# Expert steps of 256 rows instead of 128, with the first layer's weights stationary and split a step ahead, and the last norm's sums on GpSimd

## The chip, the core and the metric

The kernel runs on one core of a Trainium2 chip. Its engines run their own queues in order and meet at semaphores: TensorE (PE; PEld is its weight load), VectorE (DVE), ScalarE (ACT), GpSimd (POOL), and SyncE (SP), which mostly issues DMA. The metric is the device time of one execution in microseconds.

## What is computed

A transformer block after the norm-last scheme: attention with linear cost, layer norm, a mixture of experts (8 experts, each token goes to its best two), layer norm. 4 x 2,048 tokens of width 256, all in float32.

```python
q = relu(x @ Wq.T + bq); k = relu(x @ Wk.T + bk); v = x @ Wv.T + bv      # 16 heads of 16
q_ = concat(q * sin, q * cos); k_ = concat(k * sin, k * cos)
kv = einsum('nld,nlm->ndm', k_, v)
z = 1.0 / maximum(einsum('nld,nd->nl', q_, k_.sum(axis=1)), EPS)
x = layernorm(x + (einsum('nld,ndm->nlm', q_, kv) * z) @ Wo.T + bo)
topv, topi = top_k(x @ router_w.T, 2); w = softmax(topv)
for e in range(8):                                                       # w1: 512 x 256, w2: 256 x 512
    out += gate[:, e:e + 1] * (gelu(x @ w1[e].T) @ w2[e].T)
x = layernorm(x + out)
```

## The kernel before, in words

**Precision.** Every float32 product runs as three products of rounded numbers: each operand is split into a high part (a copy by ScalarE or GpSimd into the type fp32r) and a low part (the original less the high part, by VectorE or GpSimd); `PASSES` names high x high, high x low, low x high. So each split of an operand is two instructions, on two engines, ahead of the product.

**First half.** Tokens go through in 32 pairs of 128. TensorE makes keys, values and queries; the state of a batch is complete after its 8 pairs, so that the attention of a pair follows 9 pairs behind. Each pair then has a chain: attention product for each of its two tiles (`attend`), combination of the sine and cosine parts and division (`add_sin_part`, `normalise_attention`), transposes (`attention_transposed`), output projection (`project_out`), residual and norm, routing (`choose`, `gates`), places of rows in the experts' lists (`rank`, `positions`). GpSimd scatters each token's row twice into `expert_rows` in HBM, one region for each expert. Beside this GpSimd splits the experts' weights half by half from a raw buffer `wraw`; the last expert's are split at the change to the second half.

**Second half.** The experts work in 135 steps of 128 rows. A table made from the counts gives each step its expert and its place; a first table is made after 20 pairs, a second one when all are counted, and steps from `FULL_STEPS` on use it. SyncE gathers a step's rows from `expert_rows` into one of `NXG` = 8 buffers `xg` as soon as `freed` says that the results that lay in it have been sent. TensorE turns the rows (`rows_transposed`, a step ahead), multiplies them with the first layer (`hidden`: the rows stand still, the weights move past as 512 columns), turns the hidden rows (`hidden_transposed`) and multiplies with the second layer (`outputs`, of the step before). ScalarE copies the rows' high part, applies GELU and copies the hidden rows' high part; VectorE makes the low parts and adds the gated outputs to the rows (`gated`). GpSimd sends them to `token_rows` in HBM (`send`).

**Hooks.** The last eight pairs, and what is left of the 24th, are worked on between the expert steps: `hook(s)` gives for each step the pair and which of its six stages stands behind this step, in the code of every engine alike. The order of each queue is thus written by hand.

**Last norm.** From step 92 on, `ticks(s)` spread the second norm over the steps, four tiles of 128 tokens in three steps: SyncE loads a chunk (4 tiles, 1 MB) of `token_rows` into `z2`, VectorE adds the two rows of each token (`tile_sum`) and takes statistics, GpSimd computes the deviation's power (`deviation`), ScalarE scales and stores.

## Time and profile before

| | |
|---|---|
| median of three runs | 849.87 us (847.88 to 852.35) |
| profiled execution, span of its instructions | 841.6 us; its own total is not listed, the runs' median lies 8.3 above the span |
| TensorE busy | 793.9 us, 94% |
| VectorE, ScalarE, GpSimd busy | 566.7, 461.0, 434.3 us |
| mean granted TensorE clock | 0.984 of full |
| chain that ended last | TensorE 61% of the span, of it second layer 23%, first layer 22%, hidden transposes 7%, row transposes 4% |

A busy share is a mean over both halves. The chain is followed back from the last instruction: what stands in it sets the time where it stands.

### The profile page before, as it was taken

The page shows a single profiled execution, that of the slowest core. Times are in us where ns is not written, and L with a number is a line of the kernel's source. Part 1 is how long each engine was busy: PE and PEld are TensorE (multiplying, and loading weights), DVE is VectorE, ACT ScalarE, POOL GpSimd, SP SyncE. Part 2 cuts the span into 40 slices and gives each one's busy share as a digit, 9 for nine tenths or more (in the row PEclk, how much of TensorE's full clock was granted, in tenths as well). Part 3 has the DMA queues.
Part 4 walks back from the last instruction along what each step waited for, and adds up shares of the span by engine and source line. Part 5 has one row for each costly group of instructions (what it writes and reads, how often), then busy time and mean ns, then how long its engine had stood idle before and what let it go on. Part 6 is the DMA issues. An engine that isn't in the chain of part 4 may idle for free.

```text
span 841.6 us, 22076 instructions
## 1 busy us (share of the span) xinstructions
PE 793.9 (94%) x6684; PEld 732.7 (87%) x6684; DVE 566.7 (67%) x1816; ACT 461.0 (55%) x1044; POOL 434.3 (52%) x545
## 2 busy tenths in 40 slices
PE   4999999999999979999999999999999999999990
PEld 4887899899899969999999999989999999999980
DVE  3435788888888857766676666664444477777773
ACT  4656677667777644454444445434444446556663
POOL 3985477677677755544444454542222234444442
PEclk9999999999999989999999999999999999999995
DMA  6444033333333333323323323233322545666644
GB/s 205 160 150 127 26 102 122 113 110 108 108 103 102 98 131 117 119 90 96 99 93 96 108 88 105 87 100 107 99 78 74 179 133 193 228 226 223 220 175 173
DMA packets 56468, 106.64 MB, mean 127 GB/s; under 512 B 9261, under 2 KB 37551, under 8 KB 54448
## 3 DMA queue, kind: packets, MB, share of 16 engines
q1 hardware_dynamic: 41296, 63.25, 24.5%
q0 software_dynamic: 12624, 33.84, 11.0%
q10 hardware_dynamic: 2448, 8.26, 2.7%
q8 instruction: 58, 0.95, 0.5%
q14 instruction: 42, 0.34, 0.1%
HBM read 61.91 MB, written 44.32 MB: 126 GB/s over the span
## 4 chain that ended last, share of the span: by engine, by line
PE 61%; DMA 1%; DVE 1%; ACT 1%; issue 1%; SPq 0%; POOLq 0%; POOL 0%; ACTq 0%
PE PS L737 23%; PE PS L725 22%; PE PS L755 7%; PE PS L714 4%; PE PS L578 2%; PE PS L630 2%; DMA z<-token_rows 1%; PE PS L601 0%; PE PS L541 0%; DMA token_rows<-xg 0%; DMA expert_rows<-rows,idx 0%; PE PS L632 0%; DMA xg<-expert_rows 0%; ACT rows L862 0%; PE PS L614 0%
## 5 line engine op out<-in xcount | busy, mean ns | idle before, releaser
L1683 POOL DMA_INDIRECT token_rows<-xg x135 | 135.1, 1000 | 271.6 <-DVE xg L1407 251.1
L737 PEld LDWEIGHTS PS<-w,hT 128*128 128x128 f32 x1620 | 211.5, 190 | 12.0 <-issue 1.9
L725 PE MATMUL PS<-w,xgT 128*128 x810 | 222.0, 409 | 0.0
L737 PE MATMUL PS<-w,hT 128*128 x1620 | 217.2, 284 | 0.8 <-ACT hT L993 0.8
L725 PEld LDWEIGHTS PS<-w,xgT 128*128 128x128 f32 x810 | 143.2, 189 | 24.6
L1602 POOL DMA_INDIRECT expert_rows<-rows,idx x128 | 133.9, 1046 | 56.1 <-issue 27.8
L993 ACT ACTIVATE hT<-PS 128x512 fp32r<-128x512 f32 x135 | 80.8, 598 | 135.6 <-PE PS L755 135.6
L989 ACT ACTIVATE hg<-PS 128x512 f32<-128x512 f32 x135 | 80.7, 598 | 120.6 <-PE PS L725 120.3
L1471 DVE TENSOR_TENSOR hT<-PS,hT 128x512 fp32r<-128x512 f32 x135 | 93.4, 692 | 75.9 <-ACT hT L993 75.9
L1399 DVE TENSOR_TENSOR xgT<-PS,xgT 128x256 fp32r<-128x256 f32 x135 | 56.9, 422 | 77.8 <-ACT xgT L961 76.3
L755 PE MATMUL PS<-cst,hg 128*128 128x128 f32 x540 | 81.1, 273 | 0.0
L541 PE MATMUL PS<-wk,xs 128*128 128x264 f32 x384 | 64.3, 304 | 14.5 <-DVE wv L1340 8.4
L1407 DVE SCALAR_TENSOR_TENSOR xg<-PS,xg 128x256 f32<-128x256 f32 x135 | 65.0, 482 | 14.0 <-PE PS L737 4.9
L541 PEld LDWEIGHTS PS<-wk,xs 128*128 128x128 f32 x384 | 51.2, 192 | 21.2 <-ACT vs L853 11.8
L578 PE MATMUL PS<-sts,qs 128*128 128x272 f32 x384 | 60.7, 294 | 2.7 <-DVE sts L1091 2.4
L755 PEld LDWEIGHTS PS<-cst,hg 128*128 128x128 f32 x540 | 62.7, 141 | 0.1
L714 PE MATMUL PS<-cst,xg 128*128 128x128 f32 x270 | 52.3, 276 | 5.0 <-DMA xg<-expert_rows 4.0
L541 PE MATMUL PS<-wv,xs 128*128 128x256 f32 x384 | 56.9, 285 | 0.0
L614 PE MATMUL PS<-xs,wq 128*128 128x256 f32 x384 | 56.8, 294 | 0.0
L630 PE MATMUL PS<-wo,aT 128*128 128x264 f32 x384 | 56.5, 286 | 0.0
L578 PEld LDWEIGHTS PS<-sts,qs 128*128 128x128 f32 x384 | 52.0, 191 | 4.0 <-issue 3.0
L961 ACT ACTIVATE xgT<-PS 128x256 fp32r<-128x256 f32 x135 | 51.2, 379 | 3.4 <-PE PS L714 3.4
(179 smaller groups left out, 1272.8 us busy)
## 6 DMA issues: line engine op xcount, KB each, us to landing
xg<-expert_rows SPq DMA_DIRECT2D x135, 130.0 KB, 2.1
z<-token_rows SPq DMA_DIRECT2D x15, 1024.0 KB, 7.8
xraw<-in_xT SPq DMA_DIRECT2D x32, 256.0 KB
xtok<-in_x SPq DMA_DIRECT2D x32, 256.0 KB, 2.8
out_y<-z ACTq DMA_DIRECT2D x15, 512.0 KB, 3.4
wraw<-in_w1T SPq DMA_DIRECT2D x7, 512.0 KB, 3.9
wraw<-in_w2T SPq DMA_DIRECT2D x7, 512.0 KB, 4.0
token_rows<-xg POOLq DMA_INDIRECT x135, 2.6
```

The source lines that it names most:

```text
L541: return nc.tensor.matmul(PS[:, bank, 0:columns], xs[:, rep % 2, a, k, h * P:(h + 1) * P], weights[:, b, k, :], start=(n == 0), stop=(n == ...
L578: mm = nc.tensor.matmul(PS[:, bN + half, 0:2 * NW], qs[:, a, half, h * P:(h + 1) * P], sts[:, b, half].rearrange("p a b -> p (a b)"), star ...
L630: nc.tensor.matmul(PS[:, bank, 0:KE], aT[:, a, k, h * P:(h + 1) * P], wo[:, b, k, :], start=(n == 0), stop=False)
L714: mm = nc.tensor.transpose(PS[:, gX, k * P:(k + 1) * P], xg[:, XG_SLOTS[s % NXG], k * P:(k + 1) * P], ident)
L725: mm = nc.tensor.matmul(PS[:, gH, :], xgT[:, s % 2, a, k, :], w[:, bass.ds(e, 1), b, k * F:(k + 1) * F].rearrange("p o f -> p (o f)"), sta ...
L737: return nc.tensor.matmul(PS[:, gY, 0:D], hT[:, a, k, :], w[:, bass.ds(e, 1), b, HALF + k * D:HALF + (k + 1) * D] .rearrange("p o f -> p ( ...
L755: mm = nc.tensor.transpose(PS[:, gT, k * P:(k + 1) * P], hg[:, k * P:(k + 1) * P], ident)
L989: nc.scalar.activation(hg[:], PS[:, gH, :], ACT.Gelu, scale=2.0).then_inc(gelu_ready, 1)
L993: nc.scalar.activation(hT[:, 0].rearrange("p k t -> p (k t)"), PS[:, gT, :], ACT.Copy)\
L1471: nc.vector.tensor_tensor(hT[:, 1].rearrange("p k t -> p (k t)"), PS[:, gT, :], hT[:, 0].rearrange("p k t -> p (k t)").bitcast(F32), ALU.s ...
L1602: nc.gpsimd.indirect_dma_start(ex, bass.IndirectOffsetOnAxis(ap=idx[:, slot, h, k:k + 1], axis=0), rows[:, slot, h, k, :], None).then_inc( ...
L1683: nc.gpsimd.indirect_dma_start(yd, bass.IndirectOffsetOnAxis(ap=xg[:, XG_SLOTS[s % NXG], C_DST:C_GATE].bitcast(U32), axis=0), xg[:, XG_SLO ...
```

## The change

Expert steps have 256 rows (`TILE`), so 71 steps instead of 135, and 4 buffers `xg` of twice the size. In `hidden` the weights stand still (128 x 128 pieces) and the transposed rows move past as 256 columns, so that the hidden layer comes out already turned and `hidden_transposed` goes. The first layer's weights are no longer split in the first half: they stay whole in `w1`, and before each step ScalarE and VectorE split that step's expert into one of two buffers `w1s`, a step ahead. The second layer's weights are split by GpSimd as before, each from a place of its own. The high and low part of the hidden rows are now made from `hg` in SBUF (the low part was made from PSUM). Hooks and ticks go by half steps v = 2s, 2s + 1. GpSimd sends the two halves of a step with one send each and has the sums of all tiles but the last chunk's in its queue; statistics come four ticks behind the sums. The tails behind the experts' lists are copied from HBM. Where the diff doesn't show it, constants and places in memory change to fit.

```diff
-REGION = T + P
-STEPS = TOPK * T // P + E - 1
+TILE = 2 * P
+REGION = T + TILE
+STEPS = TOPK * T // TILE + E - 1
 EARLY_PAIRS = NPAIR - PB - 4
-FULL_STEPS = 73
+FULL_STEPS = -(-(TOPK * PAIR * EARLY_PAIRS - E * (TILE - 1)) // TILE)
...
+TAIL_HALF = 2 * LEVEL_STEPS[0] + 6
+TICK_HALVES = 3
...
+        NXG = 4
+        XG_SLOTS = (2, 3, 1, 0)
...
+            def gather(s):
+                row = nc.values_load(steps[1:2, s:s + 1], engines=[ENG.SP], min_val=0, max_val=E * REGION)
+                sp.dma_start(xg[:, XG_SLOTS[s % NXG]], ex[bass.ds(row, TILE), :].rearrange("(p h) c -> p h c", h=2))\
+                    .then_inc(s_xg[s % NXG], 16)
 
             def freed(s):
 
-                sp.wait_ge(s_y[s % NXG], s // NXG * 16)
+                sp.wait_ge(s_y[s % NXG], s // NXG * 32)
...
-                if s == LEVEL_STEPS[0] + NXG + 1:
+                gather(s)
+                if s == LEVEL_STEPS[0] + NXG:
                     sent(LEVEL_STEPS[0])
                     for n in range(LOADS):
                         load(n)
                 for c in range(LOADS, LEVEL_CH[1]):
-                    if s == LEVEL_STEPS[0] + NXG + TICK_STEPS * c:
+                    if s == LEVEL_STEPS[0] + NXG + 3 + (TICK_HALVES * (c - LOADS) + 1) // 2:
                         if c == LEVEL_CH[0]:
                             sent(LEVEL_STEPS[1])
                         load(c)
...
 
-            def hidden(s, e):
-                pe.wait_ge(xglo_ready, s + 1)
+            def hidden(s, part):
+                if part == 0:
+                    pe.wait_ge(xglo_ready, s + 1)
+                    pe.wait_ge(w1_low, s + 1)
                 if s >= 1:
-                    pe.wait_ge(gelu_ready, s)
-                m = 0
-                for k in range(KD):
-                    for a, b in PASSES:
-                        mm = nc.tensor.matmul(PS[:, gH, :], xgT[:, s % 2, a, k, :],
-                                              w[:, bass.ds(e, 1), b, k * F:(k + 1) * F].rearrange("p o f -> p (o f)"),
-                                              start=(m == 0), stop=(m == 3 * KD - 1))
-                        m += 1
+                    pe.wait_ge(gelu_ready, 2 * (s - 1) + part + 1)
+                for f in range(2):
+                    c0 = (2 * part + f) * P
+                    m = 0
+                    for k in range(KD):
+                        for a, b in ((0, 0), (1, 0), (0, 1)):
+                            mm = nc.tensor.matmul(PS[:, gH[part], f * TILE:(f + 1) * TILE],
+                                                  w1s[:, s % 2, b, k * F + c0:k * F + c0 + P],
+                                                  xgT[:, s % 2, a, k, :], start=(m == 0), stop=(m == 3 * KD - 1))
+                            m += 1
                 mm.then_inc(h_done, 1)
 
-            def outputs(s, e):
-                pe.wait_ge(hhi_ready, s + 1)
-                if s >= 1:
-                    pe.wait_ge(y_ready, s)
+            def outputs(s, e, h):
+                if h == 0:
+                    pe.wait_ge(hhi_ready, 2 * s + 2)
+                    if s >= 1:
+                        pe.wait_ge(y_ready, 2 * s)
 
...
-                pe.wait_ge(hlo_ready, s + 1)
+                if h == 0:
+                    pe.wait_ge(hlo_ready, 2 * s + 2)
                 for k in range(KF):
                     mm = part(k, 1, 0, 2 * KF + k)
-                mm.then_inc(y_done, 1)
-
-            def hidden_transposed(s):
-                pe.wait_ge(gelu_ready, s + 1)
-                if s >= 1:
-                    pe.wait_ge(hlo_ready, s)
-                for k in range(KF):
-                    mm = nc.tensor.transpose(PS[:, gT, k * P:(k + 1) * P], hg[:, k * P:(k + 1) * P], ident)
-                mm.then_inc(th_done, 1)
+                if h == 1:
+                    mm.then_inc(y_done, 1)
 
...
+                return nc.values_load(steps[0:1, s:s + 1], engines=[ENG.PE], min_val=0, max_val=E - 1)
...
+            before, now = None, expert(0)
+            for s in range(STEPS):
+                hidden(s, 0)
+                ranks(2 * s)
+                hidden(s, 1)
+                if s < STEPS - 1:
+                    rows_transposed(s + 1)
+                after = expert(s + 1) if s < STEPS - 1 else None
+                pair_part(2 * s)
+                if s > 0:
+                    outputs(s - 1, before, 0)
+                ranks(2 * s + 1)
+                if s > 0:
+                    outputs(s - 1, before, 1)
+                pair_part(2 * s + 1)
+                before, now = now, after
+            for h in range(2):
+                outputs(STEPS - 1, before, h)
...
+            def first_weights_high(s):
...
+                if s >= 2:
+                    act.wait_ge(h_done, 2 * (s - 2) + 2)
+                e = nc.values_load(steps[0:1, s:s + 1], engines=[ENG.Activation], min_val=0, max_val=E - 1)
+                nc.scalar.activation(w1s[:, s % 2, 0], w1[:, bass.ds(e, 1)].rearrange("p o f -> p (o f)"), ACT.Copy)\
+                    .then_inc(w1_high, 1)
...
+            def gelu(s, part):
+                act.wait_ge(h_done, 2 * s + part + 1)
+                if s >= 1:
+                    act.wait_ge(hlo_ready, 2 * (s - 1) + part + 1)
+                nc.scalar.activation(hg[:, 2 * part:2 * part + 2].rearrange("p k t -> p (k t)"), PS[:, gH[part], :],
+                                     ACT.Gelu, scale=2.0).then_inc(gelu_ready, 1)
+
+            def hidden_high(s, part):
+                act.wait_ge(gelu_ready, 2 * s + part + 1)
+                if s >= 2:
+                    act.wait_ge(y_done, s - 1)
+                nc.scalar.activation(hT[:, s % 2, 0, 2 * part:2 * part + 2].rearrange("p k t -> p (k t)"),
+                                     hg[:, 2 * part:2 * part + 2].rearrange("p k t -> p (k t)"), ACT.Copy).then_inc(hhi_ready, 1)
...
+
+            for s in range(STEPS):
+                if s < STEPS - 1:
+                    first_weights_high(s + 1)
+                for part in range(2):
+                    gelu(s, part)
+                if s < STEPS - 1:
+                    rows_high(s + 1)
+                for part in range(2):
+                    hidden_high(s, part)
+                pair_part(2 * s)
+                pair_part(2 * s + 1)
...
+            def first_weights_low(s):
...
+                e = nc.values_load(steps[0:1, s:s + 1], engines=[ENG.DVE], min_val=0, max_val=E - 1)
+                dve.wait_ge(w1_high, s + 1)
+                nc.vector.tensor_tensor(w1s[:, s % 2, 1], w1[:, bass.ds(e, 1)].rearrange("p o f -> p (o f)"),
+                                        w1s[:, s % 2, 0].bitcast(F32), ALU.subtract).then_inc(w1_low, 1)
...
+            def hidden_low(s, part):
+                dve.wait_ge(hhi_ready, 2 * s + part + 1)
+                if s == 1:
+                    dve.wait_ge(state_step, STATE * B)
+                nc.vector.tensor_tensor(hT[:, s % 2, 1, 2 * part:2 * part + 2].rearrange("p k t -> p (k t)"),
+                                        hg[:, 2 * part:2 * part + 2].rearrange("p k t -> p (k t)"),
+                                        hT[:, s % 2, 0, 2 * part:2 * part + 2].rearrange("p k t -> p (k t)").bitcast(F32), ALU.subtract)\
+                    .then_inc(hlo_ready, 1)
+
+            def gated(s, h):
+
+                row = xg[:, XG_SLOTS[s % NXG], h]
                 dve.wait_ge(y_done, s + 1)
-                nc.vector.scalar_tensor_tensor(out=row[:, 0:D], in0=PS[:, gY, 0:D], scalar=row[:, C_GATE:C_GATE + 1],
+                nc.vector.scalar_tensor_tensor(out=row[:, 0:D], in0=PS[:, gY, h * D:(h + 1) * D], scalar=row[:, C_GATE:C_GATE + 1],
                                                in1=row[:, 0:D], op0=ALU.mult, op1=ALU.add).then_inc(y_ready, 1)
...
+
+            for s in range(STEPS):
+                if s < STEPS - 1:
+                    first_weights_low(s + 1)
+                    rows_low(s + 1)
+                for part in range(2):
+                    hidden_low(s, part)
+                pair_part(2 * s)
+                if s > 0:
+                    for h in range(2):
+                        gated(s - 1, h)
+                pair_part(2 * s + 1)
+            for h in range(2):
+                gated(STEPS - 1, h)
...
-            def send(s):
-                pool.wait_ge(y_ready, s + 1)
+
+            def send(s, h):
+                row = xg[:, XG_SLOTS[s % NXG], h]
+                pool.wait_ge(y_ready, 2 * s + h + 1)
                 hold(pool)
-                nc.gpsimd.indirect_dma_start(yd, bass.IndirectOffsetOnAxis(ap=xg[:, XG_SLOTS[s % NXG], C_DST:C_GATE].bitcast(U32), axis=0),
-                                             xg[:, XG_SLOTS[s % NXG], 0:D], None, bounds_check=TOPK * T - 1, oob_is_err=False)\
+                nc.gpsimd.indirect_dma_start(yd, bass.IndirectOffsetOnAxis(ap=row[:, C_DST:C_GATE].bitcast(U32), axis=0),
+                                             row[:, 0:D], None, bounds_check=TOPK * T - 1, oob_is_err=False)\
                     .then_inc(s_y[s % NXG], 16)
...
+            def tile_sum(t):
+                c, q = t // NZ, t % NZ
+                if q == 0:
+                    pool.wait_ge(s_z[c % LOADS], c // LOADS * 16 + 16)
+                    if c >= SUMS:
+                        pool.wait_ge(s_out[c % SUMS], c // SUMS * 16)
+                nc.gpsimd.tensor_tensor(z[:, c % SUMS, q, :], z2[:, c % LOADS, q, 0, :], z2[:, c % LOADS, q, 1, :], ALU.add)\
+                    .then_inc(zsum_ready, 1)
+
             def tail_part(t):
-                c = chunk_at(t, NZ + 1)
+                n = tile_at(t, 0)
+                if n is not None and n < LAST_CH * NZ:
+                    tile_sum(n)
+                c = chunk_at(t, NZ + STATS_TICK)
                 if c is not None:
                     deviation(c)
...
-                send(s)
+                if s >= 2:
+                    send((s - 2) // 2, s % 2)```

How the queues change, at three places.

TensorE, at a pair's second attention product (L578 before, L563 after) and the transposes of its normalised rows (L601, L586). L725 and L714 are `hidden`, L737 and L727 `outputs`, L755 `hidden_transposed`. Before:

```order
L755 MATMUL PS<-cst,hg 128x128 x3
L578 MATMUL PS<-sts,qs 128x272 [waits o_done]
L578 MATMUL PS<-sts,qs 128x272 x5
L714 MATMUL PS<-cst,xg 128x128 [waits xglo_ready,s_xg6]
...
L737 MATMUL PS<-w,hT 128x256 [waits hlo_ready]
L737 MATMUL PS<-w,hT 128x256 x3
L755 MATMUL PS<-cst,hg 128x128 [waits hlo_ready,gelu_ready]
L755 MATMUL PS<-cst,hg 128x128 x3
L601 MATMUL PS<-cst,o 128x128 [waits la_read,at_ready]
```

After:

```order
L699 MATMUL PS<-cst,xg 128x128 x3
...
L563 MATMUL PS<-sts,qs 128x272 [waits o_done]
L563 MATMUL PS<-sts,qs 128x272 x5
L727 ISA [waits y_ready,hhi_ready]
...
L727 MATMUL PS<-w,hT 128x256 [waits hlo_ready]
L727 MATMUL PS<-w,hT 128x256 x15
L586 MATMUL PS<-cst,o 128x128 [waits la_read,at_ready]
L586 MATMUL PS<-cst,o 128x128 x3
```

Between the two stood a whole step; now there are the outputs of the same step, 24 products.

VectorE at the same place: L1051 and L1073 combine, L1062 and L1084 normalise, L1407 and L1449 are `gated`. Before:

```order
L1471 TENSOR_TENSOR hT<-PS,hT 128x512 [waits hhi_ready]
L1051 SCALAR_TENSOR_TENSOR o<-PS,cst,tcos 128x272 [waits tcos_ready]
L1058 TENSOR_SCALAR den<-o 128x32 [waits o_done]
L1060 RECIPROCAL den<-den 128x32 [waits comb_step]
L1062 TENSOR_TENSOR o<-o,den 128x4x128 [waits comb_step]
L1399 TENSOR_TENSOR xgT<-PS,xgT 128x256 [waits xghi_ready]
L1407 SCALAR_TENSOR_TENSOR xg<-PS,xg 128x256 [waits y_done]
```

After:

```order
L1424 TENSOR_TENSOR w1s<-w1,w1s 128x1024
L1432 TENSOR_TENSOR xgT<-PS,xgT 128x512 [waits xghi_ready]
L1440 TENSOR_TENSOR hT<-hg,hT 128x512 [waits hhi_ready] x2
L1073 SCALAR_TENSOR_TENSOR o<-PS,cst,tcos 128x272 [waits tcos_ready]
L1080 TENSOR_SCALAR den<-o 128x32 [waits o_done]
L1082 RECIPROCAL den<-den 128x32 [waits comb_step]
L1084 TENSOR_TENSOR o<-o,den 128x4x128 [waits comb_step]
L1449 SCALAR_TENSOR_TENSOR xg<-PS,xg 128x256 [waits y_done] x2
```

The combination now stands behind four wide instructions of its step, the split weights among them, and ahead of the step's gating.

GpSimd in the stretch of the last norm. L1683 and L1712 are `send`, L1689 and L1691 `deviation`. Before:

```order
L1689 TENSOR_SCALAR zve<-zmv 128x4 [waits zmv_ready]
L1691 TENSOR_TENSOR zrs<-zve,half_neg 128x4 [waits zpow_step]
L1683 DMA token_rows<-xg 16384x256 [waits y_ready] x3
L1689 TENSOR_SCALAR zve<-zmv 128x4 [waits zmv_ready]
L1691 TENSOR_TENSOR zrs<-zve,half_neg 128x4 [waits zpow_step]
```

After (L1728 is `tile_sum`):

```order
L1712 DMA token_rows<-xg 16384x256 [waits y_ready] x40
L1728 TENSOR_TENSOR z<-z2 128x256 [waits s_z0]
L1712 DMA token_rows<-xg 16384x256 [waits y_ready]
L1728 TENSOR_TENSOR z<-z2 128x256
L1712 DMA token_rows<-xg 16384x256 [waits y_ready]
L1728 TENSOR_TENSOR z<-z2 128x256 x2
L1712 DMA token_rows<-xg 16384x256 [waits y_ready]
L1728 TENSOR_TENSOR z<-z2 128x256 [waits s_z1]
```

Each send of a half step now has one or two sums behind it, and the next half's send behind these.

## Rows read from the trace of the kernel before

**Rows 1.** The page, busy us (share of the span) and instructions of each engine:
```profile
PE 793.9 (94%) x6684; PEld 732.7 (87%) x6684; DVE 566.7 (67%) x1816; ACT 461.0 (55%) x1044; POOL 434.3 (52%) x545
```

**Rows 2.** Chain that ended last, a plain step: start us, us, what:
```profile
358.90 1.39 PE PS L725 x6
360.29 1.44 PE PS L737 x12
361.73 0.44 PE PS L755 x4
```

**Rows 3.** Timeline around one buffer's way, end of products to next gather:
```profile
611.22 0.60 PE L755 MATMUL PS<-cst,hg 128*128 128x128 f32 x4
611.42 0.48 DVE L1407 SCALAR_TENSOR_TENSOR xg<-PS,xg 128x256 f32<-128x256 f32 x1
612.73 0.97 POOL L1683 DMA_INDIRECT token_rows<-xg  x1 [2.56 <-DVE xg L1407]
...
615.86 0.34 SPq L457 DMA_DIRECT2D xg<-expert_rows  x1
```

**Rows 4.** Waits of TensorE: who for whom, us in total, times, longest:
```profile
PE PS L714 <- DMA xg<-expert_rows: 4.0, 1, 4.0
PE PS L697 <- DVE table L1328: 1.3, 1, 1.3
```

**Rows 5.** Chain that ended last, first step and a pair's stages:
```profile
308.30 2.56 PE PS L725 x6
...
340.35 0.76 PE PS L578 x6
...
347.04 0.51 DVE o L1051
...
348.26 0.70 DVE o L1062
...
349.01 0.66 PE PS L601 x4
```

**Rows 6.** Timeline, ScalarE's GELU and the copy behind it:
```profile
704.19 0.60 ACT L989 ACTIVATE hg<-PS 128x512 f32<-128x512 f32 x1 [0.56 <-PE PS L725]
...
704.68 0.38 ACT L961 ACTIVATE xgT<-PS 128x256 fp32r<-128x256 f32 x1
```

**Rows 7.** Timeline, first and last of the eight instructions of a choice:
```profile
313.99 0.16 DVE L1112 MAX8 mx<-lg 128x8 f32<-128x8 f32 x1
...
315.35 0.16 DVE L1129 TENSOR_TENSOR dls<-dl,rstd 128x2 f32<-128x2 f32 x1
```

**Rows 8.** Groups of instructions: busy us, mean ns of one | idle before:
```profile
L1625 POOL TENSOR_TENSOR w<-wraw,w 128x256 fp32r<-128x256 f32 x56 | 44.3, 822 | 1.1
...
L1691 POOL TENSOR_TENSOR zrs<-zve,half_neg 128x4 f32<-128x4 f32 x16 | 16.9, 1057 | 1.3
...
L1393 DVE TENSOR_TENSOR w<-w_late_raw,w 128x1024 fp32r<-128x1024 f32 x1 | 1.8, 1780 | 0.0
```

**Rows 9.** VectorE's subtraction in the first half, durations ns min/median/max:
```profile
L1032 DVE TENSOR_TENSOR xs<-xraw,xs x11: 681/693/1391, 4.3 to 75.3; 128x512 fp32r<-128x512 f32 x11
```

**Rows 10.** Timeline of GpSimd, sends with their idle time before them:
```profile
354.35 0.98 POOL L1683 DMA_INDIRECT token_rows<-xg  x1 [0.30 <-issue]
...
363.09 1.08 POOL L1683 DMA_INDIRECT token_rows<-xg  x1 [0.74 <-issue]
```

**Rows 11.** DMA issues from 400 to 500: count, KB each, median us to landing:
```profile
xg<-expert_rows SPq DMA_DIRECT2D x24, 130.0 KB, 2.1
xtok<-in_x SPq DMA_DIRECT2D x4, 256.0 KB, 2.8
```

**Rows 12.** Timeline at the first loads of the last norm:
```profile
665.31 1.28 SPq L495 DMA_DIRECT2D z<-token_rows  x3
...
668.50 0.97 POOL L1683 DMA_INDIRECT token_rows<-xg  x1 [2.49 <-DVE xg L1407]
...
675.04 0.35 SPq L457 DMA_DIRECT2D xg<-expert_rows  x1
```

381 lines of the change are left out of this document (161 added, 220 removed).

## The prediction

> **What bounds the kernel now.** I read the shares of busy time first: TensorE (PE) is busy for 94% of the span, VectorE (DVE) for 67%, ScalarE (ACT) for 55%, GpSimd (POOL) for 52% [rows 1]. Then the chain that ended last, over a few plain expert steps: nothing but TensorE. A step of 128 rows is six 512-column products in 1.39 us (0.232 each), twelve 256-column products in 1.44 (0.120 each), four transposes of the hidden rows in 0.44 (0.11 each) [rows 2], and two of the gathered rows at the same 0.11: 3.49 in all. 135 of them are 471.2 us of a span of 841.6. The other work of this half (eight pairs' attention and routing) stays on TensorE as it is and cancels.
>
> A third view is needed, since the change halves the number of row buffers and doubles their size: the path of one buffer. TensorE ends the last product of a step at 611.22, VectorE takes it at 611.42, GpSimd's send starts at 612.73, and SyncE issues the next gather into a freed buffer at 615.86: 1.51 + 3.13 us [rows 3]. With eight buffers this has some 10 us to spare and shows nowhere on TensorE.
>
> **The change, part by part.**
> *Steps.* 71 steps of 256 rows. Each has 24 products of the first layer, now 256 columns wide, 24 of the second, and 4 transposes: 48 x 0.120 + 4 x 0.11 = 6.20 us [rows 2]. 71 x 6.20 = 440.2, so -31.0 against 471.2. That holds only while nobody keeps TensorE waiting, so I laid the other engines' queues beside it by hand.
>
> *Start.* TensorE waits 4.0 us for the first gather today [rows 4]; a gather twice as large, two more transposes and copies twice as wide ahead of the first product make it some 1.1 us longer. The copies of first-layer weights for step 0 are done by then.
>
> *Pairs.* Attention and routing hooks stood one per step; now one per half step, and both halves stand close together on VectorE and ScalarE, because they come behind the hidden layer's splits. Take the step with the pair's second attention product. TensorE: hidden layer to 2.88, row transposes 3.32, attention product 0.76 [rows 5] to 4.08, outputs to 6.96, and then it wants the transposes of the normalised rows. ScalarE can start its second GELU at about 3.1, 0.60 long with the next 0.49 behind it [rows 6], then the rows, then two copies: to 5.2. VectorE: the rows' low part at 4.2, two low parts of the hidden layer, the combination at 6.0; combination to normalised rows takes 1.92 (347.04 to 348.96) [rows 5]. So they are ready at 7.9, 1.0 late, and a restart costs 0.2 (transposes after a wait 0.66 rather than 0.44). Today a whole step lies between. The same count for the query split (its attention product stands at the end of the next pair's step, 0.6 late) gives 0.8. So 2.0 us for each of 8 pairs: +16. From below this could be 4 (if the splits run earlier than I placed them), from above 24.
>
> *First four steps.* In step 0 no outputs stand between the attention product and the ranking of a pair, which needs ScalarE's and VectorE's whole hidden part, the choice (1.5, 313.99 to 315.51 [rows 7]) and the combination 0.5: wanted 1.2 after the hidden layer, ready 5.1 after, 4.0 us of wait. Later in this stretch come the transposes (+1.6), the projection (+1.1) and the next pair's attention, which now waits for the positions (+2.2). Today about 1.0 is waited there. The wait of 4.0 has one more price: after the idle time before the first step, equally long, six 512-column products took 2.56 instead of 1.39 [rows 5], the granted clock being at its lower level; I add 1.9 for a second such stretch. Together +9.8; bounds 3 and 14.
>
> *Last ranking and second table.* 1.2 for the ranking. The table, for which TensorE waits 1.3 today [rows 4], is asked for with a half step less behind VectorE's chain; at most 3.5 more, I take +2.2. Together +3.4.
>
> *Split weights.* Each step VectorE gets a 1,024-column subtraction. The row of such a one has 1.78 us [rows 8], but beside GpSimd's work on late weights; two 512-column ones at their minimum are 1.36 [rows 9], so 1.2 to 1.8; ScalarE's copy is some 1.1. Register loads on both engines lie ahead of them. VectorE's step is then 1.2 + 3 x 0.69 + 2 x 0.48, or 4.3 of 6.2: hidden. If that cover were gone, each us beyond 6.2 would count 71 times.
>
> *Four buffers, sends in halves.* This I count as the largest cost. The outputs of step s end two steps and 3.3 us after its rows were transposed; step s+4 wants its rows 2.88 into the second step after that: 6.20 + 2.88 = 9.1 us from last output to gathered rows. Needed: 1.5 to the first send [rows 3], 1.3 to the second (a send directly behind another starts 0.98 + 0.30 later [rows 10]), 3.1 to the gather's issue [rows 3], and its landing: 2.1 for 130 KB, 2.8 for 256 KB of another kind, I take 2.5 [rows 11], and 0.1. That is 8.6. It just fits; plain steps stay at 6.2.
>
> In the last norm's stretch it doesn't fit. Between a step's two sends now stand one or two sums of rows (4 in 3 halves; a GpSimd operation of this size took 0.82 beside VectorE's work, so I take 0.75) and every third time a chunk's power, 1.06 and 0.3 for its addend [rows 8]; and a send behind an arithmetic instruction starts 0.74 later, not 0.30 [rows 10]. The second send comes 0.98 + 1.00 + 0.45 + 0.74 = 3.2 after the first, not 1.3: 10.5 instead of 8.6. The loads of the norm (1 MB each) slow it further: with three issued at 665.31, the send of 668.50 was followed by its gather at 675.04, 6.54 instead of 3.13 [rows 12]. A single one adds something between 0 and 3.4; I take 0.5, since it is issued some 5.5 us before the second send, so 11.0. TensorE's wait w appears in two of the steps on the loop, so 2w = 11.0 - 9.1, w = 0.95 us, in the 18 steps from the 53rd on: +17 (bounds +12.6 with no slowing, +30 with 1.7 more for each). Three loads at once come a few steps earlier: +3.5 once. Today the same slowing is hidden by eight buffers.
>
> *A rule that speaks against the sums.* One VectorE subtraction of this kind took 681 ns at the least and 1,391 at the most, over the stretch where GpSimd subtracted weights [rows 9]. The Trainium skill, SBUF — State Buffer, "Who interferes with whom", says why: a VectorE instruction with two SBUF inputs and a GpSimd instruction that reads SBUF exclude each other for their whole length. By that rule the new weight splits and the hidden split (which read PSUM before) would wait for the sums, the fourth rival below; the trace agrees as far as its maximum goes.
>
> *End.* The second send starts 1.3 later, the second gating 0.4: +1.7 before the last load; the last four sums stay on VectorE.
>
> *Nothing:* fewer weight splits in the first half lie under TensorE, which there waits for ScalarE; constants and other places in memory issue no instruction.
>
> **Sum.** -31.0 + 1.1 + 16 + 9.8 + 3.4 + 17 + 3.5 + 1.7 = +21.5. The profiled span is 841.6, so 863.1; the runs' median, 849.87, lies 8.3 above the span, which I carry over: 871.
>
> **Rivals.**
> 1. *As summed*, the buffers' round trip and the pairs' waits: 871, own range 860 to 883. Chance 0.50.
> 2. *The gathers land in time after all* (the second send is not delayed as I think, or transfers are faster), pairs' waits stay: 871 - 17 - 3.5 = 850. Speaks for it: plain steps fit by 0.5 us. Against it: the sums are in GpSimd's queue between the sends. 0.18.
> 3. *TensorE stays the bound*, faster: the hooks' waits fall under slack that I don't see and so does the ring; only start, first steps and end cost: 849.9 - 31.0 + 1.1 + 9.8 + 1.7 = 832. It decides if the second send's gather is issued within 6.6 us of the last output and the normalised rows come within 7 us of the step's start. For it speaks that today no such wait exists; against it the order of the queues. 0.15.
> 4. *VectorE becomes the bound in the last stretch*: 4.3 + the statistics of 2.7 tiles (256 wide like the gating, so 0.48 each at most) = 5.6 us a step, and up to 0.7 [rows 9] for each of three subtractions with two inputs in SBUF: 7.7 us, 1.5 over TensorE in 21 steps, 32 instead of the 17: 886. It decides from 0.6 us a step on. 0.12; the rest, 0.05, lies outside.
>
> **How the numbers follow.** A measurement here tells about 0.5%, 4.2 us, from no change. Rival 2 centres on no change with a spread of 4 us: 0.11 same, 0.03 faster, 0.04 slower. So faster 0.15 + 0.03 + 0.02 = 0.20, same 0.11 + 0.02 = 0.13, slower 0.67. The range leaves out most of rival 3 and the far end of 4: 840 to 888.
>
> **What the profile would show.** Right: TensorE waits for the gathers of rows only from the 52nd step on, about 1 us a step, with SyncE waiting for the sends' landing; waits at the transposes of attended rows of about 1 us in eight pairs, and one of about 4 us at a ranking just after the first step; the hidden products 0.12 us apart. Wrong: no wait for gathers (rival 2), a busy TensorE throughout and a span near 824 (rival 3), or TensorE waiting for the low parts of rows or weights from VectorE, whose subtractions have grown (rival 4). What would make it wrong altogether is a pace of the hidden products other than 0.12, or waits in plain steps, where the round trip fits by only 0.5 us: each 0.1 us more there would be 1 us over twenty steps.

## The result, and the profile of the changed kernel

The changed kernel takes 954.61 us (median of 4 runs, 950.86 to 960.03); the kernel before took 849.54 on the same chip. The ratio is 1.1238, 95% interval 1.119 to 1.1285: 105 us slower. I had predicted 871 us, in a range of 840 to 888. The direction was right, the size was not: four fifths of the loss were not foreseen.

The page of the changed kernel, first with the span, the busy shares and the granted clock [rows 1]:

```profile
span 955.4 us, 21892 instructions
PE 818.8 (86%) x7136; PEld 777.6 (81%) x7136; DVE 616.3 (65%) x1776; ACT 529.7 (55%) x1064; POOL 514.3 (54%) x577
PEclk9999999999999799999999999899999989998995
PE 12%; issue 11%; DMA 10%; POOL 5%; SPq 2%; DVE 2%; ACT 1%; POOLq 0%; ACTq 0%; DVEq 0%
L1712 POOL DMA_INDIRECT token_rows<-xg x142 | 173.8, 1224 | 266.8 <-DVE xg L1449 242.3
```

TensorE's share fell from 94% to 86%, but its busy time rose by 25 us, from 793.9 to 818.8. So two things happened: it waits (136.6 us of the span, 47.7 before), and its products got slower. Over the whole span no other engine is near its bound. The chain that ended last, of which TensorE had 61% of the span before, now has 12% on TensorE, 10% on DMA and 11% on plain issue (the engine waits for nothing that the profile shows). What TensorE waits for, in us in total, number of times, longest:

```profile
PE PS L699 <- DMA xg<-expert_rows: 62.2, 29, 5.3
PE PS L563 <- DVE qs L1212: 6.8, 6, 1.8
PE PS L627 <- DVE o L1073: 3.8, 1, 3.8
PE PS L714 <- DVE xgT L1432: 2.3, 2, 1.4
```

L699 is the transposes of a step's gathered rows. Before, this wait existed once, ahead of the first step [rows 4]. Now it comes 29 times, and not only in the last norm's stretch. Here are the same 120 us of both kernels, without pairs; before, the first loads of the last norm fall into them [rows 12]. First before, then after; the columns are each engine's busy us with its instructions, the granted clock, the DMA share and GB/s:

```profile
620.00:740.00 120.00, 120.00 (x825) 110.81 (x824) 73.77 (x183) 59.03 (x121) 41.13 (x45) 1.00 0.48 159
```

```profile
620.00:740.00 120.00, 109.17 (x837) 105.66 (x837) 61.47 (x96) 58.52 (x96) 40.74 (x32) 0.95 0.23 70
```

A step of 128 rows was 24 of TensorE's instructions, one of 256 rows is 52. 825 instructions are 34.4 old steps of 3.49 us. 837 are 16.1 new ones of 7.46 us, where I had counted 6.20.

**The trip of a buffer, where it is late.** The timeline of the changed kernel around one such wait:

```profile
622.37 3.05 PE L714 MATMUL PS<-xgT,w1s 128*128 128x256 f32 x24
622.57 0.88 DVE L1449 SCALAR_TENSOR_TENSOR xg<-PS,xg 128x256 f32<-128x256 f32 x2 [2.42 <-PE PS L727]
623.88 1.87 POOL L1712 DMA_INDIRECT token_rows<-xg  x1 [8.26 <-DVE xg L1449]
626.05 0.98 POOL L1712 DMA_INDIRECT token_rows<-xg  x1 [0.30 <-issue]
630.62 0.33 SPq L438 DMA_DIRECT2D xg<-expert_rows  x1
633.53 0.66 PE L699 MATMUL PS<-cst,xg 128*128 128x128 f32 x4 [1.93 <-DMA xg<-expert_rows]
```

The outputs end at about 622.4. The first send starts 1.5 later, the second another 2.2 later, the next gather into this buffer 4.6 after that, and its rows are there 2.9 later: 11.1 us, against the 8.6 that I had added up and the 9.1 that four buffers allow. Compare a trip that was in time: there the second send starts at 665.58 and the gather at 668.73, 3.15 later.

```profile
665.58 0.98 POOL L1712 DMA_INDIRECT token_rows<-xg  x1 [0.30 <-issue]
668.73 0.33 SPq L438 DMA_DIRECT2D xg<-expert_rows  x1
```

From 620 to 720 us I took all 13 pairs of second send and gather from the timeline. Eight lie 3.1 to 3.6 us apart. The other five lie 4.6, 5.3, 5.0, 3.8 and 4.9 apart, with gathers at 630.6, 647.7, 683.9, 697.8 and 712.8; TensorE's waits at the transposes end at 633.53, 650.57, 686.70, 700.50 and 715.42. Each late landing of a send is one wait, and none of the eight others cost one.

**What a wait costs on top.** Steps of the same stretch: the transposes that waited, and the 24 output products behind them.

```profile
633.53 0.66 PE L699 MATMUL PS<-cst,xg 128*128 128x128 f32 x4 [1.93 <-DMA xg<-expert_rows]
634.44 4.74 PE L727 MATMUL PS<-w,hT 128*128 x24 [0.25 <-issue]
642.25 3.11 PE L727 MATMUL PS<-w,hT 128*128 x24
650.57 0.66 PE L699 MATMUL PS<-cst,xg 128*128 128x128 f32 x4 [2.33 <-DMA xg<-expert_rows]
651.52 4.67 PE L727 MATMUL PS<-w,hT 128*128 x24 [0.30 <-issue]
700.50 0.66 PE L699 MATMUL PS<-cst,xg 128*128 128x128 f32 x4 [0.63 <-DMA xg<-expert_rows]
701.42 3.20 PE L727 MATMUL PS<-w,hT 128*128 x24 [0.26 <-issue]
```

Without a wait the 24 products take 3.11 us. After waits of 0.63, 1.06 and 1.30 us they took 3.2 to 3.25, after waits of 1.73, 1.93 and 2.33 they took 4.67 to 4.76. The granted clock of the 120 us is 0.95, which is part of the time at the lower of its two levels, 1.2 instead of 2.4 GHz. So a wait of 2 us costs about 3.6 here. The length of a wait does not settle it alone: in other stretches 24 products took 4.73 us after a wait of 1.39, and 3.02 after one of 2.80 with six attention products between.

### The profile page after: what moved, and what is told of

Its sections match the earlier page's. It is cut to its first block and busy times, and to the rows that moved or that the text cites. A ratio compares the mean times of both kernels' runs of the same rounds, so it can differ in the third digit from the quotient of the medians.

```text
span 955.4 us, 21892 instructions
## 1 busy us (share of the span) xinstructions
PE 818.8 (86%) x7136; PEld 777.6 (81%) x7136; DVE 616.3 (65%) x1776; ACT 529.7 (55%) x1064; POOL 514.3 (54%) x577
## 5 line engine op out<-in xcount | busy, mean ns | idle before, releaser
L1712 POOL DMA_INDIRECT token_rows<-xg x142 | 173.8, 1224 | 266.8 <-DVE xg L1449 242.3
L727 PE MATMUL PS<-w,hT 128*128 x1704 | 251.1, 309 | 7.5 <-issue 6.3
L727 PEld LDWEIGHTS PS<-w,hT 128*128 128x128 f32 x1704 | 237.6, 213 | 15.4 <-issue 14.3
L714 PE MATMUL PS<-xgT,w1s 128*128 128x256 f32 x1704 | 223.3, 289 | 2.3 <-DVE xgT L1432 2.3
L714 PEld LDWEIGHTS PS<-xgT,w1s 128*128 128x128 f32 x1704 | 215.4, 197 | 3.1 <-DVE xgT L1432 2.9
L1432 DVE TENSOR_TENSOR xgT<-PS,xgT 128x512 fp32r<-128x512 f32 x71 | 49.1, 691 | 148.0 <-ACT xgT L966 139.2
L1424 DVE TENSOR_TENSOR w1s<-w,w1s 128x1024 fp32r<-128x1024 f32 x71 | 89.0, 1253 | 24.0 <-issue 16.2
L699 PE MATMUL PS<-cst,xg 128*128 128x128 f32 x284 | 47.0, 290 | 62.4 <-DMA xg<-expert_rows 62.2
L1440 DVE TENSOR_TENSOR hT<-hg,hT 128x512 fp32r<-128x512 f32 x142 | 98.0, 732 | 2.4 <-ACT hT L979 2.4
L699 PEld LDWEIGHTS PS<-cst,xg 128*128 128x128 f32 x284 | 33.0, 147 | 69.1 <-DMA xg<-expert_rows 64.0
L1449 DVE SCALAR_TENSOR_TENSOR xg<-PS,xg 128x256 f32<-128x256 f32 x142 | 61.8, 477 | 39.3 <-PE PS L727 37.7
L979 ACT ACTIVATE hT<-hg 128x512 fp32r<-128x512 f32 x142 | 81.5, 627 | 0.0
L966 ACT ACTIVATE xgT<-PS 128x512 fp32r<-128x512 f32 x71 | 42.4, 596 | 70.4 <-PE PS L699 65.2
L957 ACT ACTIVATE w1s<-w 128x1024 fp32r x71 | 74.9, 1056 | 9.5 <-issue 8.1
L563 PE MATMUL PS<-sts,qs 128*128 128x272 f32 x384 | 62.2, 299 | 10.3 <-DVE qs L1212 6.8
L563 PEld LDWEIGHTS PS<-sts,qs 128*128 128x128 f32 x384 | 52.8, 193 | 14.0 <-DVE qs L1212 8.3
L854 ACT ACTIVATE rows<-xtok,pairs 128x512 f32<-128x512 f32 x64 | 49.0, 822 | 17.7 <-POOL pairs L1671 17.2
## 6 DMA issues: line engine op xcount, KB each, us to landing
xraw<-in_xT SPq DMA_DIRECT2D x32, 256.0 KB
xtok<-in_x SPq DMA_DIRECT2D x32, 256.0 KB
```

The costliest lines, as they stand in the source:

```text
L563: mm = nc.tensor.matmul(PS[:, bN + half, 0:2 * NW], qs[:, a, half, h * P:(h + 1) * P], sts[:, b, half].rearrange("p a b -> p (a b)"), star ...
L699: mm = nc.tensor.transpose(PS[:, gX, k * TILE + h * P:k * TILE + (h + 1) * P], xg[:, XG_SLOTS[s % NXG], h, k * P:(k + 1) * P], ident)
L714: mm = nc.tensor.matmul(PS[:, gH[part], f * TILE:(f + 1) * TILE], w1s[:, s % 2, b, k * F + c0:k * F + c0 + P], xgT[:, s % 2, a, k, :], sta ...
L727: return nc.tensor.matmul(PS[:, gY, h * D:(h + 1) * D], hT[:, s % 2, a, k, h * P:(h + 1) * P], w2[:, bass.ds(e, 1), b, k * D:(k + 1) * D] ...
L957: nc.scalar.activation(w1s[:, s % 2, 0], w1[:, bass.ds(e, 1)].rearrange("p o f -> p (o f)"), ACT.Copy)\
L979: nc.scalar.activation(hT[:, s % 2, 0, 2 * part:2 * part + 2].rearrange("p k t -> p (k t)"), hg[:, 2 * part:2 * part + 2].rearrange("p k t ...
```

## The experiments

The main theory, A: the ring of four buffers is shorter than its trip in every stretch, and every wait also lowers the clock. Against it stood the amount of work on GpSimd (B), a clock that falls for another reason (C), and the sums on GpSimd (D). Ratios are against the kernel before, timed on the same chip between the runs; us differences between ratios take 848 us as one.

**Six buffers, and five.**

```
-        NXG = 4
-        XG_SLOTS = (2, 3, 1, 0)
+        NXG = 6                       # five: 5
+        XG_SLOTS = (4, 5, 3, 2, 1, 0) # five: (3, 4, 2, 1, 0)
```

> The changed kernel with six buffers for gathered rows in place of four; nothing else differs. Theory A (the ring is too short for its round trip in every stretch, and each wait also lowers TensorE's granted clock): TensorE's 62 us of waits for gathered rows fall below 5, and so does part of the 0.06 of clock that is missing; 955 - 60 - about 20 = 875 us, 865 to 890. Rival B (GpSimd's queue is late by its amount of work, not by the trip's length): a deeper ring only puts the wait off, over 35 us of waits stay and the time is 920 or more. Rival C (the clock falls for another reason than these waits, the new form of the products for one): the waits go but the mean granted clock stays at 0.94, and the products still take 0.131 and 0.147 us; 895 to 905.

Measured: 888.19 us, ratio 1.0462 (1.0428 to 1.0496). Theory A, at the far end of its range.

> The changed kernel with five buffers for gathered rows in place of four. One more buffer gives the trip 6.2 us more. Theory A: the longest wait for gathered rows is 5.3 us, so one buffer more covers nearly all of them; within 5 us of the kernel with six, 870 to 890. Rival B: some 20 us of the 62 are gone, 930 us.

Measured: 889.06 us, ratio 1.0475 (1.0444 to 1.0506). One more buffer does it. With six, the span, the busy times and the waits are:

```profile
span 887.0 us, 21896 instructions
PE 780.6 (88%) x7136; PEld 750.9 (85%) x7136; DVE 622.0 (70%) x1776; ACT 524.1 (59%) x1064; POOL 516.3 (58%) x577
PE PS L586 <- DVE o L1084: 13.9, 8, 3.0
PE PS L563 <- DVE qs L1212: 10.3, 7, 2.1
PE PS L714 <- DVE xgT L1432: 9.7, 6, 2.3
PE PS L682 <- DVE table L1351: 7.1, 1, 7.1
PE PS L699 <- DMA xg<-expert_rows: 4.6, 1, 4.6
```

The span is 68.4 us shorter. 57.6 us of waits for gathered rows went; 38.2 us less were spent on the same 7,136 instructions; and some 27 us of other waits, on VectorE, came to light that had lain under the ring's. These are the waits of the pairs (L586 attended rows, L563 split query), of the second table (L682) and of the last stretch (L714). The mean clock rose from 0.94 to 0.968, where C had it stay. It can account for at most 29 of the 38.2 us: 0.94 over 955.4 us lacks 57 us of full clock, 0.968 over 887.0 lacks 28. Where the other 9 come from is not shown.

**The sums of two rows back on VectorE**, with four buffers and with six. The ticks keep their places, and the statistics follow one tick behind the sum instead of four.

```
-        STATS_TICK = 4
+        STATS_TICK = 1
...
 (VectorE, tail_part)
+                if n is not None and n < LAST_CH * NZ:
+                    tile_sum(n)
 (GpSimd, tail_part)
-                n = tile_at(t, 0)
-                if n is not None and n < LAST_CH * NZ:
-                    tile_sum(n)
```

> The changed kernel with four buffers, but the last norm's sums of two rows on VectorE again, and its statistics one tick behind the sum instead of four. Theory A: the first 740 us are untouched; of the 25 us of waits for gathered rows after 740 us the part that GpSimd's 0.9 us sums add (2 x 0.95 x some 12 steps, about 10 to 20 us) goes, VectorE is 3 us a step busier; 935 to 950. Rival D (the sums on GpSimd are the main cause of the loss, by holding up the sends in all of the last stretch and the end): below 915.

Measured: 941.56 us, ratio 1.1141 (1.1076 to 1.1206), 8 us less than the change (the two intervals overlap a little, so it is hardly clear of noise): as A has it, D refuted as the main cause.

> Six buffers, and the last norm's sums on VectorE. Theory A: once the ring is long enough the sums hide on either engine, so this is within 6 us of the kernel with six buffers alone; the end after the last step is 1 to 3 us shorter or longer. Rival E (VectorE becomes the bound in the last stretch when it makes the sums): 6 to 15 us slower than six buffers alone. Rival D again: over 10 us faster than six buffers alone.

Measured: 868.48 us, ratio 1.0236 (1.021 to 1.0263). This is 19.7 us less than six buffers alone, so A's "within 6" was wrong and D's "over 10" right; E, with VectorE as the bound, is refuted. The sums do cost, but mostly not through the ring. What they do with six buffers shows from 740 us on, first with the sums on GpSimd (to 860), then on VectorE (to 840):

```profile
740.00:860.00 120.00, 108.90 (x864) 106.66 (x863) 95.60 (x201) 79.27 (x140) 108.81 (x104) 0.97 0.59 203
```

```profile
740.00:840.00 100.00, 100.00 (x841) 100.00 (x841) 93.43 (x238) 80.37 (x141) 61.01 (x55) 1.00 0.71 242
```

On GpSimd (fifth pair of numbers) 108.81 of 120 us are busy, 91%, and TensorE idles 11.1. On VectorE the sums bring that engine to 93%, and TensorE never idles. VectorE waits for GpSimd's scale of a chunk, and one step of this stretch shows what that and the neighbourhood do (six buffers, sums on GpSimd; the waits from 740 to 870 us, then the timeline):

```profile
DVE znb L1483 <- POOL zrs L1720: 20.9, 11, 4.8
```

```profile
796.47 0.17 DVE L1483 SCALAR_TENSOR_TENSOR znb<-zmv,zrs 128x4 f32<-128x4 f32 x1 [2.42 <-POOL zrs L1720]
797.75 0.73 POOL L1728 TENSOR_TENSOR z<-z 128x256 f32<-128x256 f32 x1
...
799.50 0.68 DVE L1432 TENSOR_TENSOR xgT<-PS,xgT 128x512 fp32r<-128x512 f32 x1
800.11 2.12 DVE L1440 TENSOR_TENSOR hT<-hg,hT 128x512 fp32r<-128x512 f32 x2
800.24 3.15 PE L714 MATMUL PS<-xgT,w1s 128*128 128x256 f32 x24 [2.28 <-DVE xgT L1432]
800.47 2.35 POOL L1728 TENSOR_TENSOR z<-z 128x256 f32<-128x256 f32 x2
```

VectorE stood 2.42 us for the scale; its statistics, the weights and the row subtraction queue behind that, the last at 799.50, so TensorE waits 2.28 us. And two subtractions of VectorE that take 1.28 us elsewhere take 2.12 beside GpSimd's sums, whose own two take 2.35, where the median of all 60 is 0.75 each. From the first start to the last end these four need 2.7 us, about what they would need one behind another, 1.28 + 2 x 0.75. The Trainium skill, SBUF — State Buffer, "Who interferes with whom", says that a VectorE instruction with two SBUF inputs and a GpSimd one that reads SBUF shut each other out; these two rows agree with it.

**VectorE's pairs first** (six buffers, sums on VectorE).

```
-                for part in range(2):
-                    hidden_low(s, part)
                 pair_part(2 * s)
+                for part in range(2):
+                    hidden_low(s, part)
```

> Six buffers, the last norm's sums on VectorE (868 us), and in each expert step VectorE does the pair's part before the two subtractions of the activated hidden rows, no longer behind them (1.28 us). Theory A (after the ring, what is left are the pairs' waits, 14.9 us for the attended rows and 9.6 us for the split query, because the pair's VectorE work stands behind the step's own subtractions; and each wait also costs clock): each of the 16 waits gets up to 1.28 us shorter, some 15 us of waits go, and with them up to 8 us of lost clock; 843 to 856. Rival F (the waits are set by ScalarE or by the products of the pair, not by VectorE's order): under 3 us gained, 865 to 870. Rival G (the hidden rows' low part comes too late for the outputs): TensorE waits at the third pass of the outputs, slower than 868.

Measured: 833.34 us against 840.74, ratio 0.9908 (0.9887 to 0.9929): 28 us less than without the swap, and 0.9% under the kernel before. The attended rows' wait, 14.9 us, is 5.5, and the query's 9.6 us are gone:

```profile
PE PS L586 <- DVE o L1084: 5.5, 9, 2.2
```

TensorE's busy time falls from 776.9 to 770.1. F and G are refuted, and A had the size too small. Of the profiled executions, TensorE's idle time fell by 30 us, from 93.2 to 63.0: 19 us of these two waits, 4.0 of the table's, the rest smaller ones; the busy time gave 6.8 more.

**Every pair part a half step later** (six buffers, sums on VectorE).

```
-FIRST_GROUP = 7
+FIRST_GROUP = 8
```

> Six buffers, the sums on VectorE (868 us), and every pair's part one half step later, so that parts that stood in the middle of an expert step stand at its end and the other way round; no work is added. Theory A: the waits depend on which half a part stands in: the attended rows (14.9 us) and the query (9.6 us) get outputs of 3.1 us between the asking and the answer or lose them; the sum of the pairs' waits changes by over 5 us, either way, and the time with it. Rival H (the pairs' waits are a fixed price of three long steps in place of six short ones a pair): the same 25 us of waits, 868 within 3.

Measured: 835.45 us, ratio 0.9934 (0.9915 to 0.9952). The waits for attended rows (14.9 us) fell to 0.5 and those for the query from 9.6 to nothing; the gather after the second table now waits 7.1. The price of the pairs was that of one order, not of long steps: H is refuted.

**A narrow low part of the first-layer weights** (the changed kernel, four buffers; from the third step on it leaves out all of the low part but 8 columns).

```
-                nc.vector.tensor_tensor(w1s[:, s % 2, 1], w1[:, bass.ds(e, 1)] ...
+                n = HALF if s < 2 else 8
+                nc.vector.tensor_tensor(w1s[:, s % 2, 1, 0:n], w1[:, bass.ds(e, 1), 0:n] ...
```

> The changed kernel with its four buffers, and from the third step on VectorE subtracts only 8 of the 1,024 columns when it makes the low part of the first-layer weights (left out: the rest of that low part). Theory A: the first half's send, 1.55 us beside the subtraction, takes 1.0 again and the gating starts no later, so in the stretch without pairs (620 to 740 us, 9.0 us of waits for gathered rows) the trip is 0.6 us shorter and fits: waits there below 2 us; the long waits among the pairs stay for the most part, 930 to 948. Rival I (the subtraction does not bear on the sends): the send keeps 1.55 us and the waits in that stretch stay near 9 us; 950 or more.

Measured once: 900.78 us, where the kernel before takes 840.74. Both theories missed. The send does take 0.97 again instead of 1.55, as A said, but the waits for gathered rows from 620 to 740 us are 6.6 us after 9.0, not below 2, and the gain was larger than I expected and lies elsewhere: all waits for gathered rows went from 62.2 us to 32.8, among the pairs (340 to 580 us) from 18.3 to 5.5 and after 740 us from 25.3 to 11.4, where all of VectorE's work comes 1.1 us a step earlier. So the weight subtraction that I costed at nothing lengthens the trip, by the send and by what VectorE does behind it.

```profile
641.44 0.97 POOL L1713 DMA_INDIRECT token_rows<-xg  x1 [4.17 <-DVE xg L1450]
```

**The kernel before with fewer of its eight buffers**: four, then five and six.

```
-        NXG = 8
-        XG_SLOTS = (2, 3, 4, 0, 1, 5, 6, 7)
+        NXG = 4                    # 5, 6
+        XG_SLOTS = (2, 3, 4, 0)    # (..., 1), (..., 1, 5)
```

> The kernel before with four buffers for gathered rows in place of eight (steps of 128 rows, nothing else differs). Its buffer comes back 7.0 us after the outputs, and four buffers allow one step and the hidden product of the next, 3.49 + 1.64 = 5.1 us. Theory A: the ring's length alone costs the old form too: (7.0 - 5.1) / 4 = 0.48 us a step, x135 = 65 us and clock on top; 905 to 940. Rival J (only the longer trip of a 256-row step with its two sends is the matter): four buffers do for 128 rows, 847 to 855.

Measured once: 1104.39 us, with 194.8 us of waits for gathered rows. That the ring alone ruins the old form too is shown, but the size was off by 160 us or more. One reason is my hold: a buffer is in use from 604.64, its transposes, to 614.70, the end of its outputs, which leaves 3.9 us for a trip of 7.0, not 5.1.

> The kernel before with five of its eight buffers. A buffer is held from its transposes to the last output (604.64 to 614.70 in the trace of before: 10.1 us) and comes back 7.0 us later: 17.1 us. Four buffers give 3.49 x 4 = 14.0, five give 17.45. Theory Q, with the trip 7.0: five just fit, 848 to 870. If the trip is really 9 us or more, as the 1104 us with four buffers hint, five are 1.6 us short in a cycle of five: 0.33 a step, x135 = 45 us and clock: 890 to 940.

Measured once: 913.72 us, 45.4 us of waits. The "trip of 9 us or more" is what this says.

> The kernel before with six of its eight buffers: 20.9 us against 17.1 to 19.1 held. Any of the theories: it fits, 847 to 856; more would say that the trip reaches 11 us or more in places.

Measured once: 858.03 us against 842.41, with 12.9 us of waits, 5 of them, the longest 4.6. Not 847 to 856: even 20.9 us a round are not always enough. The trace of before did hold such a trip, and more than one: of its 18 sends from 602 to 664 us two have their gather 4.5 and 5.3 us behind them. Here is the first of the two, where [rows 3] had 3.13:

```profile
633.68 0.97 POOL L1683 DMA_INDIRECT token_rows<-xg  x1 [2.51 <-DVE xg L1407]
638.20 0.34 SPq L457 DMA_DIRECT2D xg<-expert_rows  x1
```

**Four buffers with both repairs** (sums on VectorE, pairs first).

> Four buffers as in the changed kernel, with the sums on VectorE and VectorE's pairs first (the kernel that takes 833 us, less two buffers). Theory A (four buffers are too few by themselves): the trip of 9.2 us in a plain step and some 10 to 12 among the pairs is as long as before, so 30 us or more of waits for gathered rows stay, with clock on top; 880 to 910. Rival K (the ring was short only because the pairs' waits put the gating late; with those gone four buffers do): waits for gathered rows below 12 us, under 855.

Measured: 931.21 us against 848.47, ratio 1.1014 (1.0957 to 1.1072), 56.8 us of waits for gathered rows. K is refuted. The price of two buffers is 0.111 of the ratio here, 94 us; A had the upper end at 910.

**Sums on GpSimd with pairs first, six buffers.**

> Six buffers and VectorE's pairs first, but the sums on GpSimd as in the changed kernel. Theory A (the sums cost because GpSimd is over 90% busy in the last stretch: its scale of a chunk comes late, VectorE waits for it with the steps' subtractions behind, and both engines' two-input operations get longer beside each other): the same price as with six buffers alone, 888 - 868 = 20 us; 833 + 15 to 25 = 848 to 858. Rival L (the price was an effect of the pairs' lateness and goes with it): within 5 us of 833.

Measured: 867.5 us, ratio 1.0234 (1.0208 to 1.0261); the sums cost 0.033, 28 us, more than A's 15 to 25. L is refuted.

**Pairs first and a half step later together; and pairs first with the second table's product and copy a half step later.**

> Both repairs of the pairs' waits at once: six buffers, sums on VectorE, VectorE's pairs first, every pair part a half step later. Theory A: both take away the same 25 us of waits (each left 3 to 6), so together they bring little more, 828 to 835; the second table is a half step later, which holds the gather of the 34th step up by up to 3 us. Rival M (they act on different waits and add up): 815 or less.

Measured: 850.26 us against 848.47, ratio 1.003 (1.0001 to 1.0059): A (828 to 835) and M both missed. The two don't add up, and together they are worse than either alone. TensorE waits 8.3 us for gathered rows and 4.1 for ScalarE's attended rows there; which part of the 10 us is which I did not follow up.

> The kernel of 833 us with the second table's product and its copy a half step later, everything else in place. Theory A: TensorE's 3.1 us wait for the table and the slow products behind it go; the gather of the 34th step leaves up to 3 us later and TensorE waits 1 to 4 us for it: 829 to 836, no clear difference. Rival N (the gather's lateness costs the full half step): 837 to 842.

Measured: 841.85 us against 848.47, ratio 0.9934 (0.991 to 0.9959): no better than 0.9908. On the chip of the 833 us kernel this ratio would be 835 us, which is A's range. The wait for the table (3.1 us) is gone, and the waits for gathered rows went from 5.8 to 7.1 us.

**Both sends of a step first on GpSimd** (as the four buffers with both repairs).

```
             for s in range(2 * STEPS):
+                if s >= 2 and s % 2 == 0:
+                    for h in range(2):
+                        send((s - 2) // 2, h)
...
-                if s >= 2:
-                    send((s - 2) // 2, s % 2)
```

> Four buffers, sums on VectorE, VectorE's pairs first (ratio 1.1014), and GpSimd issues both sends of a step back to back, ahead of the scatters, powers and scales that stood before and between them. Theory P (the queue between the sends lengthens the trip among the pairs and in the last stretch): waits for gathered rows fall from 56.8 to below 35 us, the stretch without pairs (8.7 us there) stays; ratio 1.04 to 1.08. Theory Q (the fixed part of the trip is what four buffers don't cover): waits stay above 48 us, ratio 1.085 to 1.11.

Measured: 930.88 us, ratio 1.1034 (1.097 to 1.1098). The waits and the time disagree on the theory: the ratio is Q's, but the waits for gathered rows did fall, from 56.8 to 29.7 us, as P said. What was won came back as another wait, since the pair's scales and scatters now stood behind the sends:

```profile
PE PS L699 <- DMA xg<-expert_rows: 29.7, 19, 4.9
PE PS L563 <- DVE qs L1212: 21.3, 7, 3.5
```

So GpSimd's queue between the sends has a part in the ring's waits, at most half (some may have gone only because TensorE now stands elsewhere), and this order did not get it for nothing. The part is all among the pairs and just behind them: from 340 to 580 us the waits for gathered rows fell from 21.6 us to nothing, from 580 to 620 from 8.4 to 3.9. In the stretch without pairs nothing changed (4.3 us, then 3.8), nor after 740 us (17.9, then 17.6), where P had them fall too.

## Why the prediction was right or wrong, by its steps

*Steps, -31.0: right.* With six buffers and the sums on VectorE, 120 us without pairs hold 1,010 of TensorE's instructions and no idle time: 19.4 steps of 6.18 us.

```profile
620.00:740.00 120.00, 120.00 (x1010) 120.00 (x1010) 81.71 (x143) 71.39 (x117) 50.49 (x41) 1.00 0.37 120
```

*Start and first four steps: right in kind.* The wait at the ranking, forecast at 4.0, is 3.8, and in the changed kernel two stretches of 24 hidden products ran at the lower clock, 5.49 and 5.33 us instead of 3.1. That is 4.6 us for both, where 1.9 was added for the second.

```profile
312.24 5.49 PE L714 MATMUL PS<-xgT,w1s 128*128 128x256 f32 x24 [1.41 <-DVE xgT L1432]
323.02 5.33 PE L714 MATMUL PS<-xgT,w1s 128*128 128x256 f32 x24
```

*Pairs, +16: the mechanism was right, the size too small.* With six buffers and the sums on VectorE TensorE waits 14.5 us for attended rows, 9.6 for the split query and 2.2 for a choice between 340 and 580 us: 26.3. The granted clock of these 240 us is 0.97. Swapping the order on VectorE alone gave back 28 us, so that is the least that this order cost.

*Last ranking and second table, +3.4:* 7.1 us of wait for the table once the ring is long enough, and 24 products behind it in 4.43.

*Four buffers, +17: this is the step that failed.* The prediction said "That is 8.6. It just fits; plain steps stay at 6.2." (Its terms add up to 8.5; the upper bound for the last norm's stretch, 30, comes out of its terms as 28 or 32. Neither matters here.) The working took each part of the trip from one row or two. The time from the second send to the gather stood in it as 3.1, from a single row [rows 3]; in the changed kernel it was 3.1 to 5.3 in thirteen trips of a plain stretch, and 4.6 to 5.3 in four of them. The first send was taken at 0.98 and took 1.55 beside VectorE's weight subtraction, a step that I had costed at nothing since it is hidden on its own engine. The gathered rows, put at 2.5, took 2.7 to 2.9 where TensorE waited for them. So even a trip whose send landed in 3.1 needed 9.1 to 9.4 us, with 9.1 allowed: there was no slack for a late one. And I looked for late trips only in the last norm's stretch, with no word on the pairs, where GpSimd's scatters and scales stand between the sends. So waits came 29 times, in all stretches. After 740 us, where the prediction put its 17 + 3.5, they are 25.3 of the 62.2 us; 4.6 are the first gather's, and the other 32 stand where it put nothing. Two buffers more take away 66 us from the changed kernel, and cost 94 us when they are taken from the best one: 17 + 3.5 was the forecast. I had named "waits in plain steps, where the round trip fits by only 0.5 us" as what would make it wrong altogether, and had left it out of the range.

*The clock behind the waits: not in the sum,* except at the start. It is at most 29 us of the 68 between four buffers and six.

*The sums on GpSimd: right cost, wrong place.* I charged them to the ring. With four buffers they are worth 8 us (the two intervals overlap); with six, 20 to 28 us, by way of GpSimd at 91%. That is near to my fourth rival's rule, but the engine that becomes the bound is GpSimd, with VectorE held up behind it, not VectorE by its own work.

*End, +1.7: right in kind, too small.* TensorE's last group of products, in the changed kernel, with six buffers and the sums on VectorE, and before:

```profile
926.94 3.33 PE L727 MATMUL PS<-w,hT 128*128 x24 [1.17 <-DVE xg L1449]
842.87 3.30 PE L727 MATMUL PS<-w,hT 128*128 x24 [1.30 <-DVE xg L1449]
819.24 1.73 PE L737 MATMUL PS<-w,hT 128*128 x12 [0.77 <-ACT hT L993]
```

From its end to the end of the span are 25.1 us (of 955.4), 23.9 (of 870.1) and 20.6 (of 841.6): 4.5 more in the changed kernel, 3.3 with the sums on VectorE.

As a ledger in us of 848: from 1.1238, the ring -66, the sums -19, VectorE's order -28, to 0.9908. The idea of the change, first-layer weights stationary with steps of 256 rows, does gain, but 8 us and not the 31 of its steps, since first steps, table, pairs and end still cost their part.

What stays open: why a send's landing takes 3.1 us once and 5 the next time. The trace shows what stands beside it. The DMA queues between a late send and its gather (642.4 to 647.6 us), then between one in time and its gather (665.6 to 668.7); packets, MB, share of 16 engines:

```profile
q0 software_dynamic: 96, 0.26, 14.2%
q8 instruction: 1, 0.02, 1.6%
```

```profile
q0 software_dynamic: 96, 0.26, 23.6%
```

Beside each of the five late sends ran one such packet of the queue for instructions, 16 KB, 1.1 to 1.6 us long and begun 0.8 to 2.1 us behind the send's start; none of the eight others had one before 2.7 us. The two late sends of the kernel before have one too, begun 1.25 and 2.5 us behind their starts. Such a packet does not always delay: the changed kernel's send at 738.44 us had one 2.05 us behind its start and was in time. That the transfer of instructions holds up the last of a send's packets is thus likely but not shown: no run changed it. The Trainium skill, DMA: Bandwidth & Descriptors, "Latency and other measured facts", gives memory's access latency as 0.2 us on average and 2 us under high load; the changed kernel moved 70 GB/s in this stretch, and no run here changed that load alone.

## What to carry to other kernels

A ring of buffers is costed with the slowest trip that the trace holds, not with the one at hand: list ten or more trips, and ask for slack of their spread. When the bytes of a ring stay the same and its pieces get twice as large, its number of steps in flight halves, and that is a change of its own. A wait on TensorE can cost more than its length: 57.6 us of waits that went took 38.2 us of busy time with them, at most 29 of it by the clock. And a reorder on another engine that lets sixteen waits end up to 1.3 us sooner was worth 28 us in all.
